# Routing the second feed-forward stages of a six-stage megakernel by expert

## The reference

```
x = x + 0.5 * moe1(ln(x))     # 8 experts, top 2, hidden 512      "moe"
x = x + gated_unit(ln(x))     #                                    "gau"
x = x + 0.5 * moe1(ln(x))     #                                    "moe"
x = x + 0.5 * moe2(ln(x))     #                                    "swiglu"
x = x + attention(ln(x))      # 16 heads of 8                      "mla"
x = x + 0.5 * moe2(ln(x))     #                                    "swiglu"

def moe2(x):                  # 8 experts of hidden 176, a shared one of hidden 352
    scores = softmax(x @ gate_w.T)
    w = scores * one_hot(top_k(scores, 2)).sum(axis=1)
    g, u = split(einsum('nh,eih->nei', x, experts_gate_up))
    out = einsum('neh,ne->nh', einsum('nei,ehi->neh', silu(g) * u, experts_down), w)
    shared = (silu(x @ shared_gate_w.T) * (x @ shared_up_w.T)) @ shared_down_w.T
    return out + sigmoid(x @ shared_expert_gate_w.T) * shared
```

## Time and profile before

| what | value |
|---|---|
| runs, median (lowest to highest) | 2124.75 us (2123.8 to 2131.32) |
| profiled execution: time, span | 2112.62 us, 2110.8 us |
| busy share PE, DVE, ACT, POOL | 86%, 59%, 33%, 28% |
| stages of the first kind | 0 to 353 us, 579 to 872 us |
| gated unit | 353 to 579 us |
| dense second kind | 872 to 1224 us, 1768 to 2102 us |
| attention | 1224 to 1768 us |
| final store | 2102 to 2111 us |
| granted TensorE clock, mean | 0.908 of 2.4 GHz |

### The profile page before, as it was taken

How to read it: one execution, slowest core, us unless ns; L and a number is a source line. 1 busy time by engine, 2 the same in 40 slices (tenths; PEclk the granted TensorE clock), 3 DMA queues, 4 the chain that set the end, 5 groups by cost and what they waited for, 6 DMA issues and landing times.

```text
span 2110.8 us, 38449 instructions
## 1 busy us (share of the span) xinstructions
PE 1813.6 (86%) x10812; PEld 1379.7 (65%) x10813; DVE 1239.8 (59%) x4206; ACT 689.7 (33%) x1279; POOL 584.9 (28%) x946
## 2 busy tenths in 40 slices
PE   3758994899844699299999969999999998999998
PEld 2547992555533699289988955555555555988987
DVE  2555885555545588566666555665655652556654
ACT  0114551222200355122232214444444442232222
POOL 2652675566257366532211010000000000000000
PEclk9758996999855799699999969999999998999999
DMA  5111212000001121100000000000000000000001
GB/s 200 38 43 51 60 50 93 25 20 21 3 29 45 57 60 55 55 21 12 19 11 11 1 0 1 1 0 0 0 0 0 0 0 1 1 0 0 0 1 41
DMA packets 61796, 54.18 MB, mean 26 GB/s; under 512 B 8579, under 2 KB 55044, under 8 KB 61189
## 3 DMA queue, kind: packets, MB, share of 16 engines
q1 hardware_dynamic: 52070, 34.20, 5.3%
q0 software_dynamic: 8192, 16.79, 2.7%
q10 hardware_dynamic: 1440, 2.10, 0.3%
HBM read 31.56 MB, written 21.50 MB: 25 GB/s over the span
## 4 chain that ended last, share of the span: by engine, by line
PE 70%; POOL 10%; DVE 8%; issue 8%; DMA 2%; SPq 1%; POOLq 1%; ACT 1%; DVEq 1%; ACTq 0%
PE bk L1007 14%; PE bk L1664 10%; PE bk L582 6%; PE bk L990 5%; PE bk L992 5%; PE bk L991 5%; POOL xs L368 4%; PE bk L1652 3%; PE bk L575 3%; PE bk L1639 2%; PE bk L1590 2%; PE bk L564 2%; PE bk L565 2%; PE bk L566 2%; DMA sb_X<-x 1%
## 5 line engine op out<-in xcount | busy, mean ns | idle before, releaser
L1007 PEld LDWEIGHTS bk<-sb_wd,sb_sc 128*128 128x128 f32 (+1 forms) x2688 | 333.0, 192 | 23.2 <-DVE sb_X L1106 3.6
L1007 PE MATMUL bk<-sb_wd,sb_sc 128*128 128x128 f32 (+1 forms) x2688 | 336.7, 275 | 0.0
L1092 DVE TENSOR_TENSOR sb_sc<-sb_sb_,bk 128x512 f32<-128x512 f32 x224 | 152.2, 684 | 230.4 <-PE bk L992 220.2
L112 POOL TENSOR_TENSOR sb_ln_ve<-sb_ln_mv,sb_eps 128x2 f32<-128x2 f32 (+1 forms) x48 | 9.4, 195 | 998.9 <-DVE sb_ln_mv L104 998.9
L1046 ACT ACTIVATE sb_sb_<-bk 128x512 f32<-128x512 f32 x224 | 133.8, 598 | 444.8 <-PE bk L992 442.0
L1918 DVE TENSOR_REDUCE sb_sc<-bk 128x2 f32<-128x512 f32 x256 | 164.6, 688 | 157.0 <-PE bk L1639 153.0
L1664 PE MATMUL bk<-sb_sa,sb_sb_ 128*32 128x256 f32 x1024 | 249.1, 387 | 0.7 <-ACT sb_sc L1813 0.7
L1826 ACT ACTIVATE sb_sa<-bk 128x512 f32<-128x512 f32 x256 | 151.1, 597 | 185.0 <-PE bk L1652 184.9
L1106 DVE SCALAR_TENSOR_TENSOR sb_X<-bk,sb_gate,sb_X 128x128 f32 (+1 forms) x576 | 161.4, 342 | 4.2 <-PE bk L1007 1.8
L582 PE MATMUL bk<-sb_w2c,sb_sb_ 128*128 x1152 | 152.2, 275 | 0.0
L368 POOL DMA_INDIRECT xs<-sb_xn,sb_send_row x128 | 128.7, 1006 | 80.3 <-DVE sb_send_row L357 44.0
(11 more groups left out here) (284 smaller groups left out, 3427.4 us busy)
## 6 DMA issues: line engine op xcount, KB each, us to landing
sb_sc<-xs SPq DMA_DIRECT2D x144, 64.0 KB, 1.9
ys<-sb_sc SPq DMA_DIRECT2D x36, 256.0 KB, 2.3
xs<-sb_xn,sb_send_row POOLq DMA_INDIRECT x128, 2.2
out<-sb_X SPq DMA_DIRECT2D x1, 2048.0 KB, 8.7
sb_sa<-w SPq DMA_DIRECT2D x1, 1792.0 KB, 14.2
sb_sc<-w SPq DMA_DIRECT2D x1, 1792.0 KB, 17.5
sb_sa<-w_gu SPq DMA_DIRECT2D x1, 1760.0 KB, 6.8
xs<-sb_zeros SPq DMA_DIRECT2D x24, 64.0 KB, 1.6
```

The costliest lines, as they stand in the source:

```text
L1007: ins = pe.matmul(bank[:, j * P:(j + 1) * P], p.hT[0:m, c % HRING, j * P:(j + 1) * P], p.wd[0:m, q * D:(q + 1) * D], start=(c == FIRST[e] ...
L1092: dve.tensor_tensor(p.hT[0:m, c % HRING, :], p.sg[0:m, c % 2, :], p.bk[2 + c % 2][0:m, :], ALU.mult)\
```

## The change

Both `swiglu` stages become routed as the `moe` stages are. Router: normalised rows go to `xq`, with two carried columns (token number, first chosen expert) as rows of 132 floats; POOL scatters them to `xs2`. While the groups are routed, the shared expert is computed for them in three chunks (`sh_up_pe`, `sh_silu_act`, `sh_product_dve`, `sh_down_pe`) and added to X (`sh_add_dve`). The rows of the `moe` stage before are gathered three groups ahead (`combine_ahead_pool`), into two pairs of buffers, and added in `sr_combine_dve`.

The expert part again has 18 units of four slot tiles. Per tile PE makes gate and up together for one expert, 352 columns with tokens as rows (`se_up_pe`, banks 0 to 3); ACT takes silu (`se_silu_act`); DVE multiplies (`se_product_dve`); PE transposes the product (`se_turn_pe`), ACT copies it, and PE multiplies down (`se_down_pe`). DVE copies the unit's output (`se_out_dve`), and POOL scatters it with four indirect DMAs (`se_back_pool`) to `y2`, to row token, or 4096 + token for the second choice, which `se_x_dve` works out from the carried columns. The next stage then loads its rows in order with plain DMAs: attention does so itself, two rows per token, group by group (`at_combine_dve`), and a new stage `out` adds the last ones and stores X group by group. `w1l` is now stored as F32 and read as fp32r, since `xq` and the slots take its space; the zero rows come from an input; the weight columns of the second kind are kept in one tensor (3520 columns).

The diff, cut to its core (the removed functions are those printed above):

```diff
+def sh_up_pe(pe, p, g, c, par):
+    n, m, q = NSC * g + c, shared_rows(c), (par + c) % 2
+    for at, bank, done, freed in ((SHARED, p.bk[q], p.sh_g, p.sh_s), (SHARED + SI, p.bk[2 + q], p.sh_u, p.sh_h)):
+        rows = slice(at + c * P, at + c * P + m)
         if not isinstance(n, int) or n >= 2:
             pe.wait_ge(freed.sem, freed.at(n - 1))
+        pe.matmul(bank[0:m, :], p.wguh[:, rows], p.xh[:, par, :], start=True, stop=False)
+        pe.matmul(bank[0:m, :], p.wgul[:, rows], p.xh[:, par, :], start=False, stop=False)
+        pe.matmul(bank[0:m, :], p.wguh[:, rows], p.xl[:, par, :], start=False, stop=True).then_inc(done.sem, 1)
...
+def sr_pe_group(pe, p, g, par, last=False):
+    sh_up_pe(pe, p, g, 0, par)
+    route_rank_pe(pe, p, g)
+    if not last:
+        sr_x_pe(pe, p, g + 1, 1 - par)
+    for c in range(1, NSC):
+        sh_up_pe(pe, p, g, c, par)
+    if not last:
+        sr_logits_pe(pe, p, g + 1, 1 - par)
+    sh_down_pe(pe, p, g)
...
+def sr_carry_dve(dve, p, g, par):
+    dve.tensor_copy(p.xq[:, par, :, D], p.token[:, bass.ds(g * TG, TG)])
+    dve.tensor_copy(p.xq[:, par, :, D + 1], p.rt_i[:, :, 0])
...
+def sr_combine_dve(dve, p, g, par):
+    dve.wait_ge(p.fetched[par].sem, p.fetched[par].at(8 * TOP * TG * (g - par + 2)))
+    for k in range(TOP):
+        dve.wait_ge(p.comb.sem, p.comb.at(TG * (TOP * g + k)))
+        combine_add_dve(dve, p, g, p.sw_taken[par][k], k)
+    dve.wait_ge(p.comb.sem, p.comb.at(TOP * TG * (g + 1)))
...
+def sr_dve_group(dve, p, g, par, after, first=False, ahead=2):
+    route_top_dve(dve, p, g, NL)
+    route_rows_dve(dve, p, g, par, sr_carry_dve)
+    if ahead >= 1:
+        route_apply_dve(dve, p, g + 1, 1 - par, p.xq, P, first)
+    sh_product_dve(dve, p, g, 0, par)
+    if ahead >= 1:
+        sr_x_dve(dve, p, g + 1, 1 - par)
+    for c in range(1, NSC):
+        sh_product_dve(dve, p, g, c, par)
+    if ahead >= 2:
+        if after:
+            sr_combine_dve(dve, p, g + 2, par)
+        route_stats_dve(dve, p, g + 2, par)
+    route_weights_dve(dve, p, g, E)
+    sh_add_dve(dve, p, g)
...
+def sr_pool_group(pool, p, g, par, after, ahead=3):
+    route_send_pool(pool, p, g, par, p.xq, p.xs2)
+    if ahead >= 2:
+        route_scale_pool(pool, p, g + 2, par)
+    if ahead >= 3 and after:
+        combine_ahead_pool(pool, p, g + 3, 1 - par)
...
+def combine_ahead_pool(pool, p, g, par):
+    if not isinstance(g, int) or g >= 2:
+        pool.wait_ge(p.comb.sem, p.comb.at(TOP * TG * (g - 1)))
+    pool.sem_inc(p.pool_passed.sem, 1)
+    pool.tensor_copy(p.take_ahead[:, par], p.out_row[:, :, bass.ds(g * TG, TG)]).then_inc(p.comb_idx.sem, 1)
+    pool.wait_ge(p.comb_idx.sem, p.comb_idx.at(g + 1))
+    pool.sem_inc(p.pool_passed.sem, 1)
+    for k in range(TOP):
+        for j in range(TG):
+            pool.indirect_dma_start(p.sw_taken[par][k][:, j * D:(j + 1) * D], None, p.ys,
+                                    bass.IndirectOffsetOnAxis(ap=p.take_ahead[:, par, k, j:j + 1], axis=0))\
+                .then_inc(p.fetched[par].sem, 16)
...
+def se_up_pe(pe, p, k, par, e, j):
+    if j == 0:
+        pe.wait_ge(p.xld.sem, p.xld.at(k + 1))
+    if not isinstance(k, int) or k >= 1:
+        pe.wait_ge(p.se_h.sem, p.se_h.at(TG * (k - 1) + j + 1))
+    c, w, out = slice(j * P, (j + 1) * P), bass.ds(e * GU, GU), p.bk[j][:, 0:GU]
+    pe.matmul(out, p.xh[:, par, c], p.wguh[:, w], start=True, stop=False)
+    pe.matmul(out, p.xh[:, par, c], p.wgul[:, w], start=False, stop=False)
+    pe.matmul(out, p.xl[:, par, c], p.wguh[:, w], start=False, stop=True).then_inc(p.se_g.sem, 1)
...
+def se_turn_pe(pe, p, k, half):
+    pe.wait_ge(p.se_h.sem, p.se_h.at(TG * k + 2 * half + 2))
+    pe.wait_ge(p.se_hc.sem, p.se_hc.at(2 * k + half))
+    for q in range(4):
+        ins = pe.transpose(p.bk[5][:, q * P:(q + 1) * P], p.gated[:, 2 * half + q // 2, (q % 2) * P:(q % 2 + 1) * P], p.ident)
+    ins.then_inc(p.se_ht.sem, 1)
...
+def se_down_pe(pe, p, k, par, half, experts):
+    pe.wait_ge(p.se_hc.sem, p.se_hc.at(2 * k + half + 1))
+    if half == 0 and (not isinstance(k, int) or k >= 2):
+        pe.wait_ge(p.se_y.sem, p.se_y.at(k - 1))
+    bank = p.bk[4 if par == 0 else 7]
+    for jj, e in enumerate(experts):
+        j = 2 * half + jj
+        for c in range(2):
+            ins = pe.matmul(bank[:, j * P:(j + 1) * P], p.gatedT[:, half, (2 * jj + c) * P:(2 * jj + c + 1) * P],
+                            p.wd[:, bass.ds((e * 2 + c) * D, D)], start=(c == 0), stop=(c == 1))
+    ins.then_inc(p.se_o.sem, 1)
...
+def se_pe_unit(pe, p, k, par, ahead=3):
+    word = sw_word(pe, p, k)
+    e = [expert_of(word, n) for n in range(2 * TG)]
+    for half in range(2):
+        if ahead >= 1:
+            for j in range(2 * half, 2 * half + 2):
+                se_up_pe(pe, p, k + 1, 1 - par, e[TG + j], j)
+        if half == 0:
+            se_turn_pe(pe, p, k, 1)
+        elif ahead >= 1:
+            se_turn_pe(pe, p, k + 1, 0)
+        se_down_pe(pe, p, k, par, half, e[2 * half:2 * half + 2])
+    if ahead >= 3:
+        se_x_pe(pe, p, k + 3, 1 - par)
...
+def se_x_dve(dve, p, k, par):
+    tiles_k = bass.ds(k * TG, TG)
+    token, first = p.sw_slots[:, par, :, D], p.sw_slots[:, par, :, D + 1]
+    dve.wait_ge(p.xhd.sem, p.xhd.at(k + 1))
+    dve.tensor_tensor(p.slot_k[:, 0], first, p.t_exw[:, bass.ds(k * TG + 1, TG)], ALU.not_equal).then_inc(p.slot_of.sem, 1)
+    dve.scalar_tensor_tensor(out=p.slot_k[:, 1], in0=first, scalar=0.0, in1=p.iota72[:, tiles_k],
+                             op0=ALU.is_lt, op1=ALU.mult).then_inc(p.slot_of.sem, 1)
+    dve.wait_ge(p.slot_of.sem, p.slot_of.at(4 * k + 2))
+    dve.scalar_tensor_tensor(out=p.slot_k[:, 2], in0=p.slot_k[:, 0], scalar=float(NTOK), in1=token,
+                             op0=ALU.mult, op1=ALU.add).then_inc(p.slot_of.sem, 1)
+    dve.wait_ge(p.slot_of.sem, p.slot_of.at(4 * k + 3))
+    dve.scalar_tensor_tensor(out=p.slot_row[:, tiles_k], in0=p.slot_k[:, 1], scalar=float(P), in1=p.slot_k[:, 2],
+                             op0=ALU.mult, op1=ALU.add).then_inc(p.slot_of.sem, 1)
+    dve.tensor_tensor(p.xl[:, par, :], p.bk[6][:], f32(p.xh[:, par, :]), ALU.subtract).then_inc(p.xld.sem, 1)
...
+def se_out_dve(dve, p, k, par):
+    dve.wait_ge(p.se_o.sem, p.se_o.at(2 * k + 2))
+    if not isinstance(k, int) or k >= 2:
+        dve.wait_ge(p.back[par].sem, p.back[par].at(32 * (k - par)))
+    dve.tensor_copy(flat(p.sw_yo[:, par]), p.bk[4 if par == 0 else 7][:]).then_inc(p.se_y.sem, 1)
...
+def se_dve_unit(dve, p, k, par, ahead=3, behind=True):
+    for half in range(2):
+        if ahead >= 1:
+            for j in range(2 * half, 2 * half + 2):
+                se_product_dve(dve, p, k + 1, j)
+        if half == 0 and behind:
+            se_out_dve(dve, p, k - 1, 1 - par)
+    if ahead >= 3:
+        se_x_dve(dve, p, k + 3, 1 - par)
...
+def se_back_pool(pool, p, k, par):
+    pool.wait_ge(p.slot_of.sem, p.slot_of.at(4 * k + 4))
+    if not isinstance(k, int) or k >= 2:
+        pool.wait_ge(p.back[par].sem, p.back[par].at(32 * (k - par)))
+    pool.sem_inc(p.pool_passed.sem, 1)
+    pool.tensor_copy(p.slot_send[:, par, :], p.slot_row[:, bass.ds(k * TG, TG)]).then_inc(p.slot_to.sem, 1)
+    pool.wait_ge(p.slot_to.sem, p.slot_to.at(k + 1))
+    pool.wait_ge(p.se_y.sem, p.se_y.at(k + 1))
+    pool.sem_inc(p.pool_passed.sem, 1)
+    for j in range(TG):
+        pool.indirect_dma_start(p.y2, bass.IndirectOffsetOnAxis(ap=p.slot_send[:, par, j:j + 1], axis=0),
+                                p.sw_yo[:, par, j, :], None).then_inc(p.back[par].sem, 16)
...
+def sw_sp(sp, p):
+    zero_rows_sp(sp, p, p.xs2, XW)
+    sp.wait_ge(p.fin.sem, p.fin.at(NFIN))
+    for k in range(2):
+        tiles_load_sp(sp, p, k, k, p.xs2, p.sw_slots, p.xld, True)
+    with sp.Fori(1, UNITS // 2) as i:
+        for m in range(2):
+            tiles_load_sp(sp, p, 2 * i + m, m, p.xs2, p.sw_slots, p.xld)
...
+def back_load_sp(sp, p, g, taken, ring, got):
+    if g >= ring:
+        sp.wait_ge(p.bcomb.sem, p.bcomb.at(TOP * TG * (g - ring + 1)))
+    for k in range(TOP):
+        sp.dma_start(taken[g % ring][k].rearrange("p (j d) -> p j d", d=D),
+                     p.y2[k * NTOK + g * W:k * NTOK + (g + 1) * W, :].rearrange("(j p) d -> p j d", p=P))\
+          .then_inc(got.sem, 16)
...
+def out_sp(sp, p, out):
+    back_wait_sp(sp, p)
+    for g in range(NG):
+        back_load_sp(sp, p, g, p.out_taken, OUT_RING, p.bgot[g % 2])
+        if g >= OUT_RING - 1:
+            out_store_sp(sp, p, g - OUT_RING + 1, out)
+    for g in range(NG - OUT_RING + 1, NG):
+        out_store_sp(sp, p, g, out)
...
+def out_store_sp(sp, p, g, out):
+    sp.wait_ge(p.bcomb.sem, p.bcomb.at(TOP * TG * (g + 1)))
+    sp.dma_start(out[:, g * TG:(g + 1) * TG, :], tiles(p, g)).then_inc(p.stored.sem, 16)
...
 
-def at_dve_element(dve, p, b, par, behind=True, ahead=2, stats=True):
+def at_combine_dve(dve, p, g):
+    dve.wait_ge(p.at_got.sem, p.at_got.at(16 * TOP * (g + 1)))
```

(9 more changed lines are left out.)

592 lines of the change are left out of this document (321 added, 271 removed).

## The result

| | changed kernel | kernel before |
|---|---|---|
| recorded runs, median (lowest to highest) | 2218.78 us (2215.42 to 2222.61) | 2127.07 us (2123.8 to 2131.32) |
| profiled execution, span | 2216.2 us | 2110.8 us |
| mean granted clock | 0.825 | 0.908 |

The ratio is 1.043, 95% interval 1.0403 to 1.0458: the change made the kernel 4% slower, where I had forecast 2099 us and a range of 2065 to 2145. The same kernel, run again in a later session, took 2084.26 us against 2112.94, a ratio of 0.987 (0.9853 to 0.9892). Both are real. A session here is a group of runs timed together on one chip, always with the kernel before among them. No chip number came back for the recorded session, and no two of the others shared a chip. So "another session" means another chip or another hour, and no run tells the two apart.

A forecast was written before the change was run, and what follows sets the result against it. PE was taken to bound the two dense second feed-forward stages. Routing them was to give -16.1 + 2.9 - 34.9 + 22.2 = -25.9 us, from the median of 2124.75 to 2099 us, range 2065 to 2145.

The forecast's parts named there:

- the expert part: Both routed stages: POOL's output scatters set the unit at 5.9 us, above PE's 5.0.
- the sum of -25.9 us: Whole kernel: first routed stage -16.1, attention +2.9, second routed stage -34.9, last stage +22.2 us.
- Units: Expert part of each routed stage: 18 units of 5.9 us, paced by POOL.
- Groups of the first stage: First routed stage's routing: POOL's sends and gathers set groups 1 to 5 at 22.5 us each.
- Chain of a group, second stage: Second routed stage's routing: the chain of waits sets 19.5 us a group, bounds 15.7 and 22.7.
- a group of 22.7 us: Routing, a rival: the clock stays low throughout, 22.7 us a group, 2124 us in all; chance 0.14.
- Start of the expert part: Both routed stages: first expert product 10.4 us after the last send ends, as in the kernel before.
- Drain: End of each routed stage: POOL's drain costs 5.4 us.
- Attention: Attention between the routed stages, now adding the routed outputs itself: +2.9 us.
- Last stage: New last stage, 6 MB at the earlier store's rate: 31.5 us, bounds 27 and 36, +22.2 us.
- the third: Expert part, a rival: DVE waits for an earlier scatter's landing before output copies; 7.4 us a unit, 2153 us; chance 0.20.
- Rival 4: Routing sends: DVE's short instructions lock POOL out of descriptor writing, adding 27 us, 2126 us in all; chance 0.06.

The follow-up runs named there:

- e5: The changed kernel, nothing edited, run again in a later session: 2084.26 us, ratio 0.9873 to the kernel before.
- e15: Changed kernel; first routed stage stores units by SP's plain DMA, POOL gathers in attention; second stage: SP loads fixed tiles. 2203.38 us.
- e16: Changed kernel; first routed stage: PE takes fixed experts; second: POOL stores each unit with one plain DMA instead of four scatters. 2165.6 us.
- e3: Changed kernel without the combination of the mixture before (POOL's gathers, DVE's additions) in the first routed stage: 2037.1 us.
- e9: Changed kernel with the shared expert left out of the second routed stage's routing: 2050.32 us.
- e18: The kernel of e9 run again in another session: 2047.85 us.
- e11: Changed kernel; in the second routed stage POOL stores each unit with one plain DMA instead of four indirect scatters: 2070.19 us.
- e10: Changed kernel with first-stage units stored by plain DMA, POOL gathering in attention, and four last-stage buffers instead of two: 2067.89 us, ratio 0.9788.
- e14: Changed kernel plus one 1 MB DRAM-to-DRAM copy issued by ACT in each unit of the second expert part: 2204.62 us.

## Why the prediction was wrong

The step that failed is the expert part: "POOL scatters each unit's output ... 5.9 us, above PE's 5.0 ... So POOL sets it". In the recorded run a unit took 8.3 and 8.0 us from scatter to scatter. The price of POOL's work was right (5.8 us apart where nothing stalls, in both stages of e5); that nothing else would stand between was not, since in the recorded session PE's results arrive late while POOL issues indirect DMAs. The rows could not show it, as the execution that they come from has no such wait and no register instruction over 0.55 us. They also mix two levels: the sum of -25.9 us was worked out on that trace, and then, though the gap of 12 us was seen, taken from a median of 2124.75, which is the level of a session that stalls; that gave 2099. Set against the trace's own 2112.62 it gives 2086.7, and e5 measured 2084.3. The account, in us:

| step | forecast | recorded | e5 |
|---|---|---|---|
| first stage: sends of group 0 at | 918.3 | 920.0 | 917.6 |
| sends of group 7 at | 1064.3 | 1092.1 | 1060.6 |
| from there to the first scatter | 33.1 | 46.3 | 42.9 |
| 18 units, to the last scatter's end | 106.2 | 146.0 | 103.1 |
| POOL's drain | 5.4 | 9.3 | 9.3 |
| second stage: start to sends 0 | 17.1 | 15.7 | 16.4 |
| seven groups | 136.5 | 133.8 | 118.2 |
| to the first scatter | 33.1 | 46.5 | 42.6 |
| 18 units | 106.2 | 141.4 | 103.7 |
| drain | 5.4 | 6.7 | 6.7 |

- **Units.** 39.8 + 35.2 us of the 131.3 by which the recorded span exceeds the forecast's 2084.9. e15 and e16 show what it hangs on in such a session. The rest is mostly the groups of the first stage (27.8), the starts of the expert parts (26.6) and the drains (5.2).
- **Groups of the first stage.** +27.8 us at the sends of group 7, beside waits of the same kind; where nothing stalls 22.6 us a group over the first five steps (forecast 22.5). This is where my reading of POOL as the bound held: e3.
- **Chain of a group, second stage.** 19.1 us recorded, 16.9 in e5, against 19.5. That the recorded one comes near is an accident: DVE waits 18.2 us there, five times, for shared products of PE that were done (L1015), and the forecast had taken the clock to be slower than it was. In e5 a group's first chunk product is at 1812.63, PE's products are 0.43 us apart until 1814.91 and 0.23 from 1816.53, so the clock is back within 4 us, earlier than the 5.5 us that I took from the earlier trace rows. It is 0.80 over the routing (0.77 recorded). The clock does change in every group, as the Trainium skill says of a kernel that waits between bursts (TensorE: Matmul & The Clock Gate, "HAM oscillation"). The price that I had set on it, a group of 22.7 us, was not met. Without the shared chunks (e9) the clock stays at 0.50.
- **Start of the expert part.** The first product was to come 10.4 us after the last send, "with the same steps"; in e5 it comes 18.0 us after (1088.64). PE's own steps are the same in both kernels: transposes of unit 0, transposes of unit 1, whose tiles land last, then products, 5.5 us before and 5.1 in e5. What differs is SP's first load of tiles. Before:

```profile
687.00 4.00 SPq L487 DMA_DIRECT2D xs<-sb_zeros  x8
...
698.81 1.12 PE L554 MATMUL bk<-sb_tables,sb_sc 128*128 128x128 f32 x4 [18.10 <-DMA sb_sc<-xs]
```

  and e5:

```profile
1066.89 1.12 DVE L1015 SCALAR_TENSOR_TENSOR sb_X<-bk,sb_sh_gate,sb_X 128x128 f32<-128x128 f32 x4 [2.31 <-PE bk L951]
...
1073.53 3.98 SPq L417 DMA_DIRECT2D xs<-sb_zeros  x8
...
1079.98 22.01 SPq L430 DMA_DIRECT2D sb_w1l<-xs  x20
...
1083.51 1.11 PE L1088 MATMUL bk<-sb_tables,sb_w1l 128*128 128x128 f32 x4 [16.60 <-DMA sb_w1l<-xs]
...
1088.64 0.66 PE L1099 MATMUL bk<-sb_wguh,sb_xh 128*128 x1
```

  Before its first load SP writes eight rows of zeros. In the kernel before they went out beside the last sends, and the load 1.5 us behind these (695.37 against 693.89). In e5 they come only after the sends, and the load 9.3 us behind (1079.98 against 1070.66): SP waits for DVE's table of rows, and this stands in DVE's order behind the last group's shared additions. With the shared expert left out of the second routing (e9, e18), 35.7 and 35.6 us lie between the last group's sends and the first scatter instead of 42.6, near the 33.1 of the forecast. This is a mis-sized term, 9.5 to 9.8 us a stage in e5, 7.6 of it ahead of the first product, and needs no stall.
- **Drain.** 9.3 and 6.7 us at the two stages' ends, not the 5.4 of the earlier trace rows, in e5 as in the recorded run. The 5.4 came from a place where POOL's last DMA lay 178 us back; now the last of 72 scatters stands just ahead. With plain DMAs (e11) it is 3.1.

```profile
1293.76 1.80 POOL L2258 MEMSET sb_sa<- 128x2048 f32 x1 [9.32 <-POOLq L63]
```

- **Attention** +2.7 (forecast +2.9): right. **Last stage** 32.6 (31.5): near, by luck. I had reasoned that the DMA engines are full there; they are 0.67 busy (0.69 in e5), and with four buffers instead of two the stage took 25.9 us (e10). What holds it is load, then add, in turn, since a buffer is loaded again only when its group is added. Chain of waits, recorded run:

```profile
2183.97 3.43 DMA sb_sb_<-y
...
2187.49 1.15 DVE sb_X L1384 x4
...
2193.22 3.85 DMA sb_sb_<-y
```

- **Sum.** Where nothing stalls the change is worth 28.7 us (2112.94 to 2084.26) and I had 25.9. That is near by luck: in e5 the groups of the second stage took 18.3 us less than forecast and the units 5.6 less, while the two starts took 19.3 more and the drains 5.2. Of the rivals, the third is the one nearest in size, not in place: in the recorded first expert part DVE waits 5.2 us, once, before an output copy. Rival 4 fell: the sends of `xq` took 0.97 us each (median, at most 1.87) with DVE's short instructions beside them. So what I had drawn from the Trainium skill (SBUF — State Buffer, 'The "DVE blocks DMA" trap (SWDGE)') cost nothing that these runs show; whether DVE's short instructions are of the kind that it speaks of was not tested.

Not shown:

- What delays the semaphores of PE's results in such a session, and why SP's and PE's register instructions slow down with it.
- Whether the chip or the hour decides if a session stalls.
- Whether the recording has a part in it. In the four traces that stall fewer semaphore updates are on record (17,300 to 17,800, in e5 24,400), also in stages without a stall. No execution is known to have gone unrecorded, so no run tells whether the recording slows the core or suffers with it.
- Why the `moe` stages' routing, with its sends back to back, waits so little: 3.8 us, once, in the recorded run, 14.2 in e15, nothing in e14 and e16.
- That the kernel before loses its 15 us in such a session to its own gathers in the first dense stage. It is likely and was not seen.

## What to carry to other kernels

Before explaining a slowdown by the code, run the unedited kernel again in another session, if possible on another chip, and give every experiment a control stage inside the same kernel. See to it that the trace from which you forecast and the time to which you add the sum come from the same level. Where consumers go on together long after their producer's last instruction, look at when its semaphore moved, and at who was issuing meanwhile; here it was POOL's indirect DMAs, and a plain store per unit took the stall away in that part. At a stage's start, count what stands in order ahead of the first load, not only what the first product itself needs.

## What the runs showed of the hardware

- In three of nine sessions, beside POOL's indirect DMAs, the semaphores that announce PE's results to ACT and DVE moved late, by 8.6 us and more in the group shown (177 waits in four traces), and some register instructions of PE and SP took 0.7 us instead of 0.04 to 0.06. The changed kernel took 2219 us in one of them and 2084 in one without, the kernel before 2127 and 2113. Chip and hour are not told apart.
- In such a session one plain DMA of POOL per unit does not do it (5.35 us a unit), four indirect ones do (7.7). Kind and number are not told apart.
- POOL's drain took 9.3 us at the first stage's end and 6.7 at the second's behind its scatters, stalled or not, 3.1 behind a plain DMA (e11), and 5.4 before, with no DMA of its own for 178 us.
- TensorE's clock changed in every group of a routing with shared chunks between its waits (0.80 on average in e5) and stayed at its lower level, 0.50, in one without them (e9).
